# First products moved behind the last variance, segments turned one unit sooner, centrings moved into the recurrence

## The reference

```
x = x + rwkv_and_moe(layernorm(x))        # 8 experts
x = x + ffn9(layernorm(x))                # 9 paths, hard choice, own layer norm
x = x + random_features(layernorm(x))     # 16 heads of 8, 32 features per head
x = x + ffn9(layernorm(x))
x = x + segments(layernorm(x))            # 16 heads, segments of 64 tokens
x = x + tree(layernorm(x))                # 255 routers, 256 leaves
x = x + linear_recurrence(layernorm(x))
x = x + tree(layernorm(x))
layernorm: (x - mean) / sqrt(var + 1e-5)
random_features: Q,K = x Wq, x Wk; phi(z) = exp(z.proj - max) * exp(-|z|^2/2) + 1e-6
                 out = (phi(Q) (phi(K)^T V)) / (phi(Q) sum phi(K)) Wo + bo
segments: per segment softmax(q k^T / sqrt 8) v over the own 64 keys,
          + 1/4 of the same over every 4th key of each of the segments -2, -1, +1, +2
          (where there is one); then Wo + bo
linear_recurrence: k = exp(x Wk + b), kv = k v, r = sigmoid(x Wr + b)
                 u1, u2 = running sums of kv, k decayed by lam each token
                 out = ((u1 + g kv) / (u2 + g k + 1e-6) * r) Wo + bo
```

## Time and profile before

| | |
|---|---|
| time, median of 3 | 1256.6 us |
| the profiled execution: its time, its span | 1258.29 us, 1256.2 us |
| busy: TensorE, VectorE, ScalarE, GpSimd | 91%, 74%, 65%, 18% |
| mean granted clock of TensorE | 0.95 |
| granted clock of the segment stage, 782 to 1070 | 0.88 |

### The profile page before, as it was taken

The page is one execution under the profiler, slowest core; times in us unless marked ns, Lnnn a source line. Parts: engine busy times, 40 slices in busy tenths (PEclk is TensorE's granted clock), DMA queues, the critical chain, the costliest instruction groups (busy, mean ns, idle before and its releaser), DMA issues.

```text
span 1256.2 us, 20246 instructions
## 1 busy us (share of the span) xinstructions
PE 1139.7 (91%) x7444; PEld 639.9 (51%) x7452; DVE 930.1 (74%) x1515; ACT 815.3 (65%) x1300; POOL 230.7 (18%) x330
## 2 busy tenths in 40 slices
PE   7899899999999999799998998798888888898787
PEld 3343344444444344377763453476666676463354
DVE  4967788777777767577775666697888896577766
ACT  6967555556556745645676547486777775868674
POOL 1000000000000011100000012486867675000000
PEclk9999999999999989989999999698899988999899
DMA  6000122122211000000000000000000000000002
GB/s 170 1 0 1 55 59 68 63 59 59 67 59 63 5 1 0 10 2 2 2 1 1 0 1 9 0 2 2 2 2 3 15 2 3 9 1 1 0 1 67
DMA packets 26362, 27.19 MB, mean 22 GB/s; under 512 B 4171, under 2 KB 17308, under 8 KB 26268
## 3 DMA queue, kind: packets, MB, share of 16 engines
q1 hardware_dynamic: 25936, 25.91, 6.9%
q10 hardware_dynamic: 332, 0.01, 0.0%
HBM read 23.30 MB, written 2.62 MB: 21 GB/s over the span
## 4 chain that ended last, share of the span: by engine, by line
PE 63%; DVE 17%; ACT 14%; issue 6%; DMA 0%; SPq 0%; DVEq 0%; ACTq 0%
PE psum L730 8%; PE psum L741 8%; PE psum L733 4%; PE psum L990 3%; PE psum L87 3%; PE psum L1937 3%; PE psum L962 3%; PE psum L1606 3%; PE psum L1947 2%; PE psum L1380 2%; DVE N L2126 2%; ACT ln_std L116 2%; ACT ln_std L114 2%; DVE arena L2117 2%; DVE arena L2116 2%
## 5 line engine op out<-in xcount | busy, mean ns | idle before, releaser
L769 ACT ACTIVATE arena<-psum 128x512 f32<-128x512 f32 x128 | 69.5, 595 | 114.5 <-PE psum L730 114.5
L730 PE MATMUL psum<-arena,weights 128*128 128x512 f32 x256 | 122.3, 601 | 1.7 <-DVE N L128 1.0
L741 PE MATMUL psum<-arena,weights 128*128 128x512 f32 x256 | 120.3, 593 | 0.0
L627 DVE SCALAR_TENSOR_TENSOR arena<-diff,vecs,N 128x512 f32<-128x512 f32 x128 | 95.2, 747 | 0.0
L2037 ACT ACTIVATE N<-N 128x1024 f32<-128x1024 f32 x64 | 67.8, 1059 | 41.7 <-DVE N L2126 41.4
L689 DVE SCALAR_TENSOR_TENSOR arena<-arena,psum 128x512 f32<-128x512 f32 x64 | 44.0, 688 | 62.5 <-PE psum L741 62.5
L1937 PE MATMUL psum<-arena 32*128 32x128 f32 x1024 | 84.6, 310 | 4.8 <-ACT arena L2005 4.8
L1937 PEld LDWEIGHTS psum<-arena 32*128 32x128 f32 x1024 | 71.1, 210 | 33.7 <-issue 18.7
L1947 PE MATMUL psum<-ident,N 128*128 128x128 f32 x512 | 77.2, 299 | 10.2 <-ACT arena L2033 9.9
L2033 ACT ACTIVATE arena<-psum 128x1024 f32<-128x1024 f32 x64 | 65.4, 1022 | 30.6 <-PE psum L1947 30.2
L730 PEld LDWEIGHTS psum<-arena,weights 128*128 128x128 f32 x256 | 48.6, 192 | 62.4 <-issue 58.0
(11 more groups left out here) (332 smaller groups left out, 2484.5 us busy)
## 6 DMA issues: line engine op xcount, KB each, us to landing
arena<-tw_rows SPq DMA_DIRECT2D x64, 256.0 KB, 3.1
out_dram<-arena SPq DMA_DIRECT2D x8, 256.0 KB, 3.6
arena<-in_L_attn_a_x_dram SPq DMA_DIRECT2D x3, 512.0 KB, 7.2
weights<-in_L_attn_a_eWk_dram SPq DMA_DIRECT2D x1, 1024.0 KB, 5.8
arena<-in_L_attn_a_x_dram SPq DMA_DIRECT2D x2, 256.0 KB, 4.1
weights<-in_L_attn_a_eWr_dram SPq DMA_DIRECT2D x1, 512.0 KB, 9.8
tw_rows<-arena SPq DMA_DIRECT2D x2, 128.0 KB, 2.7
tw_rows<-arena SPq DMA_DIRECT2D x1, 256.0 KB, 3.4
```

The lines of the kernel that those rows point to most:

```text
L627: op = nc.vector.scalar_tensor_tensor(mixed[:, n % 4, a, :], k.diff[:, q % 2, :], k.vec((f"cm_k{e}", f"cm_r{e}")[a]), before, ALU.mult, AL ...
L730: op = nc.tensor.matmul(k.bank[2 * (n % 2) + h][:], k.eWk[:, e, h * P:(h + 1) * P], mixed[:, n % 4, 0, :], start=True, stop=True)
L741: op = nc.tensor.matmul(k.bank[4 + n % 2][:], k.eWv[:, e, h, :], ks[:, (2 * (n % 2) + h) * CH:(2 * (n % 2) + h + 1) * CH], start=(h == 0), ...
L769: op = nc.scalar.activation(kr[:, h * CH:(h + 1) * CH], k.bank[2 * (n % 2) + h][:], ACT.Relu)
```

## The change

Feed-forward: in the first turn `hidden(0, 1)` is issued behind `scores(0, 0)`, ahead of the first transposes; on ScalarE its copies stand ahead of the first `choice`.

Random features: the functions for projection and norms are shared with the LN's feed. `project(0)` stands at c = 7 (behind the last centring), `norms(0)` at c = 9 (behind the last variance); ScalarE copies them behind deviations 5 and 6. The second copy of the weights is at c = 3 instead of 5. `scores` 0 and 1 and `values(0)` wait for the banks that they write instead of for the whole LN.

Segments: eight first products in the order of `FIRST`, each as soon as its bank is free: K, Q, V of batch 0 and K of batch 1. The first K half is copied inside the LN. `ln_sq` and `ln_std` are cleared by GpSimd. Turning, weighed products, `heads`, output and addition each come a unit sooner, the values a unit later; the loop ends a unit sooner.

Recurrence: the centrings and variances of the last LN stand in `output(2)` between its identity products and its W_o products; squares and deviations on ScalarE stand behind `weigh_product(3)`.

```diff
@@ -995,8 +995,10 @@
                     turned(*before)
-                hidden(it, c, first and c == 0)
+                if not first:
+                    hidden(it, c)
                 if first and c == 0:
+                    hidden(it, 0, True)
                     pe.wait_ge(k.ln_out, normed)
@@ -1004,6 +1006,8 @@
                 scores(it, c)
+                if first and c == 0:
+                    hidden(it, 1)
                 if not (first and c == 0 or last and c == 1):
@@ -1040,9 +1044,13 @@
             for c in range(2):
-                if not (first and c == 0):
+                if first and c == 0:
+                    hidden(it, 0)
+                    hidden(it, 1)
+                else:
                     choice(*((it - 1, 1) if c == 0 else (it, 0)))
-                hidden(it, c)
+                if not first:
+                    hidden(it, c)
@@ -1141,6 +1149,13 @@
                 nc.tensor.matmul(out_to[c][:], k.ident[:], k.X[:, at(b, c)], start=True, stop=False)
+            if b == B - 2:
+                pe.wait_ge(k.lr_r, 2 * B)
+                for c in range(4):
+                    pe.wait_ge(*(((k.lr_kv, 2 * B - 1), (k.lr_kv, 2 * B))[c < 2]))
+                    after.center(pe, c)
+                for c in range(2):
+                    after.variance(pe, c)
             for c in range(2):
@@ -1219,13 +1227,14 @@
                 exponentials(b + 1)
+            if b == B - 1:
+                for c in range(4):
+                    after.square(act, c)
+                for c in range(2):
+                    after.deviation(act, c)
             if b >= 1:
                 add(b - 1)
-        for c in range(4):
-            after.square(act, c)
         over(B - 1)
-        for c in range(2):
-            after.deviation(act, c)
         add(B - 1)
@@ -1535,7 +1544,40 @@
+    def project(pe, c):
+        if c >= 1:
+            pe.wait_ge(k.fv_nm, c)
+        if c >= NCH + 4:
+            pe.wait_ge(k.fv_x, c - NCH - 3)
+        w = P if c < NCH else 0
+        nc.tensor.matmul(other[:], wT[:, w:w + P], k.Y[:, columns(c)], start=True, stop=True).then_inc(k.fv_proj, 1)
...
+    def norms(pe, c):
+        pe.wait_ge(k.fv_sq, c + 1)
+        for t in range(4):
+            op = nc.tensor.matmul(other[:, t * H:(t + 1) * H], sq[c % 2][:, t * P:(t + 1) * P], k.fv_heads, start=True, stop=True)
+        op.then_inc(k.fv_norm, 1)
...
+    def keep_project(act, c):
+        act.wait_ge(k.fv_proj, c + 1)
+        if c >= 2:
+            act.wait_ge(k.fv_score, 2 * c - 2)
+        nc.scalar.activation(qs[c % 2], other, ACT.Copy, scale=DK ** -0.5)
+        nc.scalar.activation(sq[c % 2], other, ACT.Square, scale=(0.5 / DK) ** 0.5).then_inc(k.fv_sq, 1)
...
+    def keep_norms(act, c):
+        act.wait_ge(k.fv_norm, c + 1)
+        if c >= 2:
+            act.wait_ge(k.fv_off, 2 * c - 2)
+        nc.scalar.activation(nm[c % 2], other[:, 0:4 * H], ACT.Copy).then_inc(k.fv_nm, 1)
...
+        if c == 7:
+            pe.wait_ge(k.fw_copied, 3)
+            pe.wait_ge(k.ln_out, k.ln_done - NCH + 1)
+            project(pe, 0)
+        if c == 9:
+            norms(pe, 0)
@@ -1563,32 +1605,23 @@
-        if c == 5:
+        if c == 3:
...
-    normalize((turn_weights, keep_weights))
-    normed = k.ln_done
+    def keep_first(act, c):
+        if c == 5:
+            keep_project(act, 0)
+        if c == 6:
+            keep_norms(act, 0)
...
+    normalize((turn_weights, keep_weights, keep_first))
+    normed, logs = k.ln_done, k.ln_logged
...
-            if c >= 1:
-                pe.wait_ge(k.fv_va, c)
+            pe.wait_ge(*((k.fv_va, c) if c >= 1 else (k.ln_logs, logs)))
@@ -1599,6 +1632,8 @@
                 pe.wait_ge(k.fv_arg, n - 1)
+            else:
+                pe.wait_ge(k.ln_out, normed - (2, 0)[n])
             for t in range(4):
@@ -1665,10 +1700,6 @@
-        pe.wait_ge(k.fw_copied, 3)
-        pe.wait_ge(k.ln_out, normed)
-        project(0)
-        norms(0)
@@ -1887,20 +1902,35 @@
-    PROJ = {0: 0, 2: 1, 3: 2, 4: 3, 7: 4, 11: 5}
+    PROJ = {0: 0, 1: 1, 3: 2, 4: 3, 7: 4, 11: 5}
...
-        return (n // 16 + 1) * 6 + PROJ[n % 16] if n < N - 16 and n % 16 in PROJ else None
+        return (n // 16 + 1) * 6 + PROJ[n % 16] if 2 <= n < N - 16 and n % 16 in PROJ else None
...
-        return n // 4 if n < N and n % 4 == 1 else None
+        return n // 4 if n < N and n % 4 == 2 else None
...
-        return (n - 14) // 8 if n >= 14 and n % 8 == 6 else None
+        return (n - 13) // 8 if n >= 13 and n % 8 == 5 else None
...
+    FIRST = ((1, 0, 0), (1, 1, 1), (0, 0, 4), (0, 1, 5), (2, 0, 7), (2, 1, 6), (1, 2, 2), (1, 3, 3))
...
+    def first_in(dve, n):
+        w, c, bank = FIRST[n]
+        dve.wait_ge(k.sg_proj, n + 1)
+        nc.vector.tensor_scalar(own((k.sg_K, k.sg_V)[w - 1], 0, c), k.bank[bank].rearrange("p (s n) -> p s n", n=SEG),
+                                k.vec(("bk", "bv")[w - 1]), None, ALU.add).then_inc(k.sg_first, 1)
...
+    def keep_first(dve, c):
+        if c == 6:
+            first_in(dve, 0)
...
+    normalize((lambda pe, c: None, keep_first))
+    normed, logs = k.ln_done, k.ln_logged
...
-        last = []
+        last = [(k.sg_first, 3)]
@@ -1908,10 +1938,11 @@
             pe.wait_ge(k.sw_in, 7 * 16)
-            pe.wait_ge(k.ln_out, normed)
-            for i in range(6):
-                nc.tensor.matmul(k.bank[i][:], k.sg_w[:, (1, 2, 0)[i // 2], :], k.Y[:, i % 2 * CH:(i % 2 + 1) * CH],
-                                 start=True, stop=True).then_inc(k.sg_proj, 1)
+            ready = ((k.ln_out, normed - 3), (k.ln_out, normed - 2), (k.ln_logs, logs - 1), (k.ln_logs, logs), None, (k.ln_logs, logs - 2), (k.ln_out, normed - 1), (k.ln_out, normed))
+            for (w, c, bank), bank_free in zip(FIRST, ready):
+                if bank_free is not None:
+                    pe.wait_ge(*bank_free)
+                nc.tensor.matmul(k.bank[bank][:], k.sg_w[:, w, :], k.Y[:, c * CH:(c + 1) * CH], start=True, stop=True).then_inc(k.sg_proj, 1)
@@ -1922,11 +1953,15 @@
             b, u, half = n // T2, n // 2, n % 2
+            if n == T2 // 2:
+                pe.wait_ge(k.sg_q, 4)
             if n % T2 == 0:
-                pe.wait_ge(k.sg_q, 4 * b + 4)
+                pe.wait_ge(k.sg_q, 4 * b + 4 if b else 2)
                 pe.wait_ge(k.sg_kd, 4 * b + 4)
-            if n < 2:
-                pe.wait_ge(k.sg_first, 2 * n + 2)
+            if n == 0:
+                pe.wait_ge(k.sg_first, 2)
+            elif n == 1:
+                pe.wait_ge(k.sg_kv, 2)
             else:
@@ -1978,13 +2013,13 @@
         first()
-        for n in range(N + 7):
+        for n in range(N + 6):
             if n < N:
                 scores(n)
+            if 0 <= n - 3 < N:
+                turned(n - 3)
             if 0 <= n - 4 < N:
-                turned(n - 4)
-            if 0 <= n - 5 < N:
-                weighed(n - 5)
+                weighed(n - 4)
             if project_at(n) is not None:
@@ -2006,19 +2041,19 @@
-        def project(p):
+        def project(p, bank=other):
...
-                nc.scalar.activation(own((k.sg_K, k.sg_V)[i // 2], b, i % 2), other.rearrange("p (s n) -> p s n", n=SEG), ACT.Identity,
+                nc.scalar.activation(own((k.sg_K, k.sg_V)[i // 2], b, i % 2), bank.rearrange("p (s n) -> p s n", n=SEG), ACT.Identity,
...
-                act.wait_ge(k.sg_quarters, 1)
+                act.wait_ge(k.sg_quarters, 3)
@@ -2050,14 +2085,16 @@
-            act.wait_ge(k.sg_proj, 5 + c)
+            act.wait_ge(k.sg_proj, 3 + c)
...
-        for n in range(N + 7):
-            if n >= 13 and n % 8 == 5:
-                heads((n - 13) // 8)
-            if 0 <= n - 4 < N:
-                turned(n - 4)
+        project(6, k.bank[2])
+        project(7, k.bank[3])
+        for n in range(N + 6):
+            if n >= 12 and n % 8 == 4:
+                heads((n - 12) // 8)
+            if 0 <= n - 3 < N:
+                turned(n - 3)
@@ -2089,9 +2126,13 @@
+        pool.wait_ge(k.ln_logs, logs)
+        nc.gpsimd.memset(k.ln_sq[:], 0.0).then_inc(k.sg_quarters, 1)
...
+        pool.wait_ge(k.ln_out, normed)
+        nc.gpsimd.memset(k.ln_std[:], 0.0).then_inc(k.sg_quarters, 1)
@@ -2139,20 +2180,17 @@
-        for i in range(4):
-            dve.wait_ge(k.sg_proj, i + 1)
-            nc.vector.tensor_scalar(own((k.sg_K, k.sg_V)[i // 2], 0, i % 2), k.bank[i].rearrange("p (s n) -> p s n", n=SEG),
-                                    k.vec(("bk", "bv")[i // 2]), None, ALU.add).then_inc(k.sg_first, 1)
-        for v in (k.ln_sq, k.ln_std):
-            nc.vector.memset(v[:], 0.0)
+        first_in(dve, 1)
...
+        first_in(dve, 4)
+        first_in(dve, 5)
...
-            if n >= 15 and n % 8 == 7:
-                add((n - 15) // 8)
+            if n >= 14 and n % 8 == 6:
+                add((n - 14) // 8)
```

(13 more changed lines are left out.)

31 lines of the change are left out of this document (removed).

## The result

The changed kernel has a median of 1219.8 us (1218.1 to 1224.1, 4 runs) against 1257.3 us before (1256.0 to 1259.2, 4 runs): a ratio of 0.9706, 95% interval 0.9677 to 0.9734. The forecast was 1235 with a range of 1225 to 1246. The direction and most steps were right; one term had the wrong sign and put the time outside the range.

The account below looks back on a forecast made before the run. TensorE, with 63% of the chain of waits, was taken to set the time in most stages but not in the seams; -4.5 - 11.8 + 3.1 - 1.1 - 6.3 - 0.7 = -21.3 from 1256.6 gave 1235, range 1225 to 1246.

Parts of the forecast that it names:

- Features: Random-feature start: project and norms move into the LN's last steps, first maximum 5.05 earlier, 0.5 given back; -4.5 us.
- Segments, start: Segment stage up to unit 6: eight dense early products, first maximum 10.4 sooner; -11.8 us altogether, bounds -15 and -8.
- Feed-forward: Both calls: second hidden products fill the gap before the turning; -0.7 us together, bounds -2.4 and +1.
- Tail and recurrence: Segments' end, one step less before the last turning: -1.1 us; recurrence, centrings and variances filling TensorE's gap: -6.3.
- Segments, a unit sooner: Steady segment stage: lost TensorE lead +3.0, waits for the addition +7.7, credits -3.5 and -4.1; sum +3.1 us.
- the credit side: Steady segment stage savings: two old stalls of projections behind an addition go, -3.5; no transposes after heads, -4.1.
- the bound of -7: Steady segment stage's lower bound, if stalls at half clock, most of VectorE's 23.6 us of score waits, shrink.
- Rival A: Segment stage: half-clock stalls shrink, since `shift` no longer waits for a turning; 8 more gained, 1227 us; chance 0.18.
- Rival C: Segment stage: turnings waiting for GpSimd take TensorE's lead, the clock falls more often; slower, 1270 us; chance 0.07.

Follow-up runs that it names:

- e4: Changed kernel with the addition of an output to X ahead of the next unit's maxima instead of behind its subtraction; 1208.9 us.
- e6: Changed kernel with the sooner segment steps put back a unit later and the next batch's second projection back in unit 2; 1231.0 us.
- e3: Changed kernel with one wait more: VectorE's subtraction of unit n waits for the turning of unit n-3; 1220.6 us.
- e1: Kernel before with only turning, weighed product, heads, values, output and addition each a unit sooner; 1256.8 us.
- e9: e6 with the last projection of the next batch moved from unit 11 to unit 10; 1222.8 us.
- e10: Kernel before with only the last projection of the next batch moved from unit 11 to unit 10; 1256.1 us.
- e2: Changed kernel with turning, weighed product, heads, values, output and addition put back a unit later, second projection left in unit 1; 1244.7 us.
- e12: e4 with 6 small unread 128x128 copies on ScalarE ahead of each of the first seven heads' copies; 1225.0 us.
- e11: e4 with 3 small unread 128x128 copies on ScalarE ahead of each of the first seven heads' copies; 1216.2 us.
- e7: e4 with value transposes moved from unit 6 of each 8 to unit 4, one projection from 4 to 6; 1226.2 us.

## Why the forecast was too small

**Features: right.** The first maximum was forecast at 528.7 in the time of before and came at 528.4. I gave back 0.5 for low clock that did not come, and the second unit gained 0.3 more.

**Segments, start: right, and somewhat low.** First scores were put at 786.0 and came at 786.1, the copies and the clearing in the order described. I had GpSimd's clearing at 2.2; it took 1.81, as good as VectorE's 1.76. The ratio of 1.96 that the Trainium skill has for an add ("GPSIMD Engine Reference", section 3.1) would have made it 3.4; it does not carry over to a clearing here. The clock fell as expected, but TensorE was back at full rate at 793.8, which is 800.4 in the time of before where I had 806; that is the 2.7 us between -11.8 and -14.5.

**Feed-forward: wrong by 1.2,** in the clock of the second call; inside the bounds given.

**Tail and recurrence: right,** -1.1 and -6.4. The products of W_o were put at 1181.0 and came at 1181.0 (1147.38 + 33.6), the variance of chunk 2 at 1187.5 and came at 1187.95.

**"Segments, a unit sooner": the step that failed.** It was +3.1 and measured -11.4. Its costs were largely right. The seven waits of TensorE for an addition came (1.76 each; +7.7 forecast, 10.3 when e4 removes them), and so did the short waits for GpSimd. What failed is the credit side. The sum put what the sooner order saves at half rate at nothing and left it to the bound of -7; the runs show 13.8 us less of TensorE's busy time for the same passes. And the credit "where `heads` releases the weighed product (the 2.10 us wait at 850.75) no transposes of 0.59 follow before the scores, seven times, -4.1" priced what follows the wait and took the wait itself as given. In the three batches with queries these waits of 2.10 to 2.39, two of them with one of 0.82 ahead, became single ones of 1.08; behind the old ones TensorE ran at half rate each time, behind the new ones never. From unit 12 to unit 16 of these batches after takes 16.4 to 17.2 us and e6 19.2 to 19.6, which is 8 of the 11. I also left out VectorE's waits for the turning in the subtraction (5.0 us in 8 waits before, none after).

**Rival A** named the nearest result (1227, chance 0.18) and rightly that the stalls at half clock shrink, with a reason that e3 does not bear out, and was still 7 too high. The time that came lies where I had left a chance of 0.03, better than 1224. **Rival C** went the wrong way. Its 17 waits for GpSimd of up to 1.2 us came in, TensorE's idle time in the stage did not fall, and the clock still rose to 0.99. The rule of the Trainium skill that stood beside it ("TensorE: Matmul & The Clock Gate", Part 1: throttled by default, released by activity) does not tell these kernels apart by how idle the stage is. TensorE idles 34.2 us in the stage of e1 at a clock of 0.98 and 19.8 in that of e9 at 0.92. What does differ between before and after is how the idle time is cut up: before has waits of 1.73 to 2.39 for copies of ScalarE, after has none above 1.25 but those of 1.76 for an addition.

What stays open is why the sooner order keeps full rate, and how much of e9's remaining 3 us is that. The waits are a part of it, but the same wait is followed by full rate in one place and by half rate in the next: that of 1.76 for an addition by full rate in five of seven cases in after, the pair of about 1.0 and 0.76 by half rate in three of six in e9 and e10. No run here forces or removes half rate without moving a wait too.

## What to carry to other kernels

When a step moves by one unit in an order written out by hand, list for every engine what now stands ahead of it, in its own unit and in the one before; a part of the gain or loss can be a neighbour on another engine's queue, here the query copies ahead of the heads' copy. Price a stall of TensorE with the passes behind it: waits of 0.8 and 2.1 us cost 4.5 us more here than waits of 1.0 and 0.8 in their place in the two batches of e9 where those were followed by full rate, and 1.0 us more in the third, where they were not. Compare busy and idle time of the engine before calling two gains the same: e9 and after are 3 us apart and got there by different ways. Two users of one PSUM bank in one unit can be dear (19.6 us in e2), and an addition that frees a bank should stand as early as its product allows: that one move gave 10.9 us.

## What the runs showed of the hardware

In units 6 to 63 of the 14 profiles, "followed by half rate" means that one of the four groups of passes that begin with the one that waited took over 1.15 times its time at full rate (1.16 us for scores, 1.09 for a turning, 0.65 for weighed products). Each time TensorE had run at full rate up to the wait.

- Waits for the heads' copy: of 1.94 to 2.39 us, 16 of 16 were followed by half rate (before, e2, e6, e10, e12); of 1.49 to 1.84, one of five (e11, e12); of 0.98 to 1.32 with no other long wait right behind, none of 22.
- Waits of 1.76 for an addition: 13 of 38. Waits of 1.73 for the copy of the turned block: 6 of 10. Waits of 2.28 to 2.31 for a copy of a projection out of bank 7: 2 of 4 (e2 yes, e1 no); of 2.84 for the query copies: three of three (e7). Waits for GpSimd of 1.16 to 1.32: 6 of 29; of 0.98 and 0.99: none of 12. So the length alone does not decide.
- A wait of 1.02 or 1.15 followed by one of 0.76 with a turning between them (e9, e10): 3 of 6.
- TensorE's idle time in the stage does not order the granted clock: 34.2 us at 0.98 (e1), 29.2 at 0.99 (after), 26.8 at 0.91 (before), 19.8 at 0.92 (e9).
- GpSimd clears 128x2048 fp32 in 1.81 to 1.83 us, VectorE in 1.76.
